# The Gram matrix from high and low fp32r parts, and LN1's normalisation on ScalarE from the second batch on

## The chip, the cores and the metric

The kernel runs on one core of a Trainium2 chip. The metric is the device time of one execution in microseconds (us). The numbers of the profile come from one execution recorded by the hardware profiler.

## The reference

Inputs are x (8 batches of 2048 tokens of 256 features), an attention with 8 heads of 64, a gated feed-forward block and six modulation rows per batch. All is float32.

```
sa, ca, ga, sb, cb, gb = (silu(c) @ wmod), six rows of 256 per batch; ga, gb pushed to |.| >= 0.25
h   = layernorm(x) * (1 + ca) + sa                        # LN1
q, k, v = split(h @ w_qkv + b_qkv)
s   = einsum('bhld,bhle->bhde', q, k) / 8                 # 64 x 64 per head, summed over the tokens
o   = v @ softmax(s)   per head;  o = o @ w_fc + b_fc + h
x   = x + ga * (layernorm(o) * gamma + beta)
h   = layernorm(x) * (1 + cb) + sb                        # LN2
xr, xk = mixes of h with h of the token before
x   = x + gb * sigmoid(xr W_r') * (relu(xk W_k')**2 W_v')
```

The attention is over features, so all that the scores need of a batch is the Gram matrix G = Z^T Z of z, the normalised x with a last column that stands for the bias. Scores, softmax and the product with w_fc are folded into one 256 x 256 matrix M per batch, and the attention output of a token is z M.

## The kernel before, in words

A batch is cut in four tiles of 512 tokens (`CH = 4`), a tile in four blocks of 128 (`NT = 4`). Every engine has an instruction list of its own, written out by hand: a prologue with batch 0's Gram matrix, `row_steps(b)` for b = 0 to 6, `last_row(7)`. `row_steps(b)` does attention and feed-forward of batch b, and between them the LN1, transposes, Gram matrix, scores and M of batch n = b + 1. There is no planner: the order in each list is the schedule, and semaphores tie the lists together.

What the change touches, in the order of the data:

- VectorE `stats_a` takes the statistics of a tile of x, GpSimd `rstd_a` (through `layernorm_factors`, L445 to L461) makes mean and 1/std, VectorE `make_z` (L884) writes z, in two buffers. Tiles 0 and 1 of batch n + 1 are normalised at the end of `row_steps(b)`, tiles 2 and 3 in the next one.
- TensorE `turn_and_gram` transposes z into the banks `tr` (L1249) and adds the tile's part to the bank `gram` (L1256): per block an f32 matmul of 256 columns and one of 128, since the lower left quarter follows from symmetry. ScalarE copies the transposes (`copy_z_t`, L618).
- After the fourth tile ScalarE copies three quarters of G (`copy_gram`), TensorE transposes one (`turn_gram`, L1349), ScalarE copies that (`copy_gram_low`), and `gram_q` (L1359) begins the scores. Then come the softmax on VectorE, `wv_attn` (L1376; it needs `wv_aug` from GpSimd's L494 to L504), and `make_m` (L1385, added up on VectorE at L1015).

What lies around it: `attention(b, j)` (L1274) fills the banks `att`; ScalarE `squares` sums them, GpSimd `rstd_o` (L476, L478) makes 1/std, VectorE `make_x2` (L894, L899) makes the new x, `stats_2` (L905) its statistics, GpSimd `rstd_2` the factors of LN2, ScalarE `make_z2` (L699) normalises, TensorE `turn_z2` (L1291) transposes, ScalarE `copy_h2` (L661) modulates, VectorE `mix` (L919, L923) mixes, and `ffn_r` (L1307), `ffn_k` (L1324), `take_r` (L671), `take_k` (L680 to L684), `low_k` (L932), `ffn_out` (L1140 to L1142, three fp32r products) and `gate_o` (L941) follow. `attention(b, 2)` waits for `t_done` of tile 1, `turn_z2(b, j)` also for the copies of the next z tile, since both use the banks `tr`. GpSimd's list of a middle batch has, in this order, `rstd_o(b,0)`, two DMA issues, `rstd_2(b,0)`, `prep_wv(n)`, `rstd_o(b,1)`; in the prologue `centre_wv(0)` waits for `row8_b_ready`, which the end of VectorE's `rows_b` (L838 to L857) sends.

Of the kernel before, what the change touches and what calls it, by code (L numbers as in the profile page):

```python
# [24 lines left out]
F32 = mybir.dt.float32  # L25
# [8 lines left out]
def adaln_block(nc, x, w_qkv, b_qkv, w_fc, b_fc, gamma, beta, w_r, w_k, w_v, mu_r, mu_k, c, wmod, out):  # L34
# [19 lines left out]
    with ExitStack() as ctx:  # L54
# [25 lines left out]
        def att_banks(j, alone):  # L80
# [7 lines left out]
        neg_half, half, quarter, minus_one, eps_att = (  # L88
            sb(n, [P, NT]) for n in ("neg_half", "half", "quarter", "minus_one", "eps_att"))
# [43 lines left out]
        z = sb("z", [P, 2, NT, D])  # L133
        z_t = sb("z_t", [P, CH, KD, CT])
# [112 lines left out]
        ag_a_step = sem("ag_a_step")  # L247
        rs_a_ready = sem("rs_a_ready")
# [3 lines left out]
        z_t_ready = sem("z_t_ready")  # L252
        x2_rowed = [sem(f"x2_rowed{j}") for j in range(CH)]
# [170 lines left out]
        def _(pool):  # L424
            def build_constants():
# [11 lines left out]
                nc.gpsimd.memset(quarter[:], 0.25).then_inc(const_ready, 1)  # L437
                nc.gpsimd.memset(eps_att[:], EPS_ATT).then_inc(const_ready, 1)
# [3 lines left out]
                nc.gpsimd.memset(z[:, :, :, LAST:D], 1.0).then_inc(const_ready, 1)  # L442
                pool.wait_ge(const_ready, 10)

            def layernorm_factors(i, st, ag, st_done, ag_step, ready, eps):  # L445
# [66 lines left out]
            def row_steps(b, first, far):  # L512
# [73 lines left out]
        def _(act):  # L586
# [27 lines left out]
            def copy_z_t(b, j):  # L614
                i = CH * b + j
                for h in range(KD):
                    act.wait_ge(z_turned, 2 * i + h + 1)
                    nc.scalar.activation(z_t[:, j, h], tr[h][:], ACT.Copy).then_inc(z_t_ready, 1)  # L618

            def copy_gram(b):  # L620

                act.wait_ge(z_used, CH * (b + 1))
                nc.scalar.activation(g_sb[:, 0], gram[:, 0:D], ACT.Copy)
                nc.scalar.activation(g_sb[:, 1, P:D], gram[:, D:D + P], ACT.Copy).then_inc(g_up_ready, 1)

# [77 lines left out]
            def row_steps(b, first):  # L703
# [26 lines left out]
                copy_gram_low(n)  # L730
# [4 lines left out]
                make_z2(b, 3)  # L735
                exps(n)
# [47 lines left out]
            row_steps(0, True)  # L784
            with act.Fori(1, B - 1) as b:
                row_steps(b, False)
# [4 lines left out]
        def _(dve):  # L791
# [67 lines left out]
            def centre_fc():  # L859
# [4 lines left out]
                nc.vector.tensor_scalar(fc_mean[:], fc_mean[:], 1.0 / D, None, ALU.mult).then_inc(fc_step, 1)  # L864
                dve.wait_ge(fc_step, 2)
# [11 lines left out]
            def make_z(b, j, first=False):  # L877
# [8 lines left out]
                ins.then_inc(z_ready, 1)  # L886

# [130 lines left out]
            def row_steps(b, first, far):  # L1018
# [18 lines left out]
                mix(b, 0)
# [29 lines left out]
                if far:  # L1067
                    stats_a(n + 1, 3)
# [427 lines left out]
```

## Time and profile before

| what | value |
|---|---|
| median of 3 runs | 707.41 us (706.69 to 708.01) |
| the profiled execution's own time | 705.8 us |
| its span, first to last instruction | 704.2 us |
| PE busy in the stretches 0 to 75, each middle batch, 647 to the end | 65.6 of 75; 81.0 of 82; 45.2 of 57 us |
| distance of the same instruction in two middle batches | 82.05 us |
| mean granted TensorE clock | 0.991 |
| VectorE, ScalarE, GpSimd busy in a middle batch's 82 us | 63.5, 48.4, 47.7 us |

Matmuls overlap in the pipeline, so a group's duration in the lists is longer than its pace. The pace is the distance from one start to the next. An idle time in brackets is that of the engine ahead of the row, with what ended it.

### The profile page before, as it was taken

How to read it: one execution, taken by the hardware profiler on the slowest of the kernel's cores; microseconds unless marked ns; L12 is line 12 of the kernel's file. 1: busy time of each engine (PE TensorE's matmuls, PEld its weight loads, DVE VectorE, ACT ScalarE, POOL GpSimd, SP SyncE). 2: the span in 40 equal slices, each digit the busy share in tenths (PEclk: the TensorE clock that was granted, in tenths of full speed). 3: DMA queues.
4: the chain of work that ended last, by engine and by line, in shares of the span. 5: the costliest groups of instructions: out<-in, count | busy, mean ns of one | idle time of the engine just before them, and what ended most of it. 6: DMA issues, size and time to landing. Idle time of an engine off the chain costs nothing.

```text
span 704.2 us, 11623 instructions
## 1 busy us (share of the span) xinstructions
PE 676.1 (96%) x3584; PEld 548.0 (78%) x3584; DVE 524.8 (75%) x1030; ACT 392.8 (56%) x871; POOL 389.5 (55%) x809
## 2 busy tenths in 40 slices
PE   7988999999999999999999999999999999998896
PEld 6767787978788887887879787888878878786665
DVE  4784898768878687868877688786878588467853
ACT  1434575556655475474755565554754747546552
POOL 5172885567275663586455672756635864326530
PEclk9999999999999999999999999999999999999999
DMA  9759255675846375573926657563755629616225
GB/s 317 220 166 210 90 158 91 130 163 113 194 86 146 120 158 118 97 177 89 217 77 133 162 117 184 89 151 111 165 116 92 124 57 199 117 29 153 30 31 89
DMA packets 90984, 93.02 MB, mean 132 GB/s; under 512 B 4224, under 2 KB 89000, under 8 KB 90960
## 3 DMA queue, kind: packets, MB, share of 16 engines
q0 software_dynamic: 33264, 33.03, 31.9%
q1 hardware_dynamic: 55344, 55.97, 24.9%
q10 hardware_dynamic: 2352, 3.73, 1.5%
q8 instruction: 11, 0.18, 0.1%
q14 instruction: 13, 0.11, 0.1%
HBM read 42.84 MB, written 33.10 MB: 108 GB/s over the span
## 4 chain that ended last, share of the span: by engine, by line
PE 34%; POOL 26%; issue 21%; DVE 9%; ACT 6%; DMA 2%; POOLq 1%; DVEq 0%; SPq 0%
PE work L1307 6%; PE att L1274 5%; PE gram L1256 5%; PE work L1324 4%; POOL x L483 4%; POOL ag L461 2%; ACT z L699 2%; POOL wv_aug L494 2%; PE tr L1249 2%; POOL ag_a L461 2%; DVE t_buf L894 2%; DVE mx L923 2%; POOL wv_aug L497 2%; PE gram L1385 2%; POOL rs_o L478 2%
## 5 line engine op out<-in xcount | busy, mean ns | idle before, releaser
L1274 PE MATMUL att<-m_sb,z_t 128*128 128x256 f32 x496 | 112.9, 381 | 8.4 <-DVE t_buf L894 7.6
L1274 PEld LDWEIGHTS att<-m_sb,z_t 128*128 128x128 f32 x496 | 92.4, 190 | 24.9 <-issue 13.7
L1324 PE MATMUL work<-mx,w_k_t 128*128 128x512 f32 x236 | 106.2, 592 | 0.0
L1307 PE MATMUL work<-w_r_t,mx 128*128 128x256 f32 x464 | 105.0, 379 | 0.0
L894 DVE SCALAR_TENSOR_TENSOR t_buf<-att,rs_o,g_row 128x256 f32<-128x256 f32 x124 | 51.4, 477 | 64.4 <-POOL rs_o L478 64.4
L1307 PEld LDWEIGHTS work<-w_r_t,mx 128*128 128x128 f32 x464 | 86.1, 190 | 10.4
L699 ACT ACTIVATE z<-x,ag 128x256 f32<-128x256 f32 x128 | 66.5, 598 | 48.6 <-POOL ag L471 48.6
L1256 PE MATMUL gram<-z 128*128 128x256 f32 (+1 forms) x512 | 89.7, 329 | 0.0
L449 POOL TENSOR_TENSOR ag<-st 128x4 f32<-128x4 f32 x32 | 18.6, 582 | 125.5 <-DVE st L905 125.5
L652 ACT ACTIVATE sq<-att 128x256 f32<-128x256 f32 x124 | 45.9, 382 | 72.4 <-PE att L1274 72.4
L1256 PEld LDWEIGHTS gram<-z 128*128 128x128 f32 x512 | 80.4, 192 | 6.7
L923 DVE SCALAR_TENSOR_TENSOR mx<-t_buf,mu_col,h2t 128x512 f32<-128x512 f32 x120 | 82.2, 748 | 1.1
L1324 PEld LDWEIGHTS work<-mx,w_k_t 128*128 128x128 f32 x236 | 44.9, 190 | 44.0 <-issue 42.5
L1140 PE MATMUL work<-wvf_lo,k_hi 128*128 128x256 f32 x248 | 77.1, 311 | 0.0
L1142 PE MATMUL work<-wvf_hi,k_lo 128*128 128x256 f32 x248 | 69.7, 281 | 0.0
L1141 PE MATMUL work<-wvf_hi,k_hi 128*128 128x256 f32 x248 | 69.5, 280 | 0.0
L932 DVE TENSOR_TENSOR k_lo<-work,k_hi 128x512 fp32r<-128x512 f32 x61 | 41.9, 690 | 36.6 <-ACT k_hi L684 35.5
L671 ACT ACTIVATE y<-work 128x512 f32<-128x512 f32 x58 | 34.5, 595 | 59.4 <-PE work L1307 59.3
L483 POOL DMA_DIRECT2D x<-in_L_attn_x_dram x32 | 55.0, 1821 | 0.0
L884 DVE TENSOR_SCALAR z<-x_in,ag_a 128x255 f32<-128x255 f32 x128 | 50.0, 453 | 6.1 <-POOL ag_a L461 4.1
L661 ACT ACTIVATE h2t<-tr,mod_now 128x512 f32<-128x512 f32 x64 | 46.2, 776 | 12.1 <-PE tr L1291 12.1
L510 POOL DMA_DIRECT2D out_dram<-y x29 | 39.3, 1355 | 18.5 <-DVE y L941 17.6
(176 smaller groups left out, 1373.8 us busy)
## 6 DMA issues: line engine op xcount, KB each, us to landing
x_in<-in_L_attn_x_dram SPq DMA_DIRECT2D x32, 512.0 KB, 4.9
x<-rows SPq DMA_DIRECT2D x32, 512.0 KB, 3.5
x<-in_L_attn_x_dram POOLq DMA_DIRECT2D x32, 512.0 KB, 9.4
out_dram<-x SPq DMA_DIRECT2D x31, 512.0 KB, 4.8
out_dram<-y POOLq DMA_DIRECT2D x29, 512.0 KB, 6.0
rows<-row_scratch SPq DMA_DIRECT2D x16, 128.0 KB, 4.9
rows<-row_scratch SPq DMA_DIRECT2D x8, 256.0 KB, 3.8
wqkv_sb<-in_L_attn_w_qkv_dram ACTq DMA_DIRECT2D x1, 1536.0 KB, 10.0
```

The costliest lines, as they stand in the source:

```text
L483: nc.gpsimd.dma_start(x2[:, j], x_v[b, j], accum_op=ALU.add).then_inc(x2_filled[j], 16)
L699: ins = nc.scalar.activation(z2[:, t], x2[:, j, t], ACT.Identity, bias=ag_2[:, s, 1, t:t + 1], scale=ag_2[:, s, 7, t:t + 1])
L884: ins = nc.vector.tensor_scalar(z[:, j % 2, t, 0:LAST], x_in[:, j, t, 0:LAST], ag_a[:, j, 3, t:t + 1], ag_a[:, j, 7, t:t + 1], ALU.subtrac ...
L894: ins = nc.vector.scalar_tensor_tensor(t_buf[:, t], att_banks(j, alone)[t // 2][:, (t % 2) * D:(t % 2 + 1) * D], rs_o[:, s, t:t + 1], g_ro ...
L923: ins = nc.vector.scalar_tensor_tensor(dst[:, h], dif[:, h], mu_col[:, n, h:h + 1], prev[:, h], ALU.mult, ALU.add)
L1140: mm(dst, s_hi, m_lo, start=start, stop=False)
L1141: mm(dst, s_hi, m_hi, start=False, stop=False)
L1142: return mm(dst, s_lo, m_hi, start=False, stop=stop)
L1256: ins = mm(gram[:, k * D:(k + 1) * D - k * P], z[:, j % 2, t, k * P:(k + 1) * P], z[:, j % 2, t, k * P:D], start=(j == 0 and t == 0 and k ...
L1274: ins = mm(att_banks(j, alone)[q][:, (t % 2) * D:(t % 2 + 1) * D], z_t[:, j, k, t * P:(t + 1) * P], m_sb[:, k], start=(k == 0), stop=(k == ...
L1307: ins = mm(r_banks(alone)[q][:, (t % 2) * D:(t % 2 + 1) * D], mixed(j, alone)[0][:, ch, tile], w_r_t[:, ch], start=(ch == 0), stop=(ch == ...
L1324: ins = mm(k_banks(alone)[dh][:], w_k_t[:, ch, rows_dh], mixed(j, alone)[1][:, ch], start=(ch == 0), stop=(ch == KD - 1))
```

## The change

TensorE now forms G in two fp32r products, z_hi^T z_hi and z_lo^T z_hi, with all 256 columns in each. z is doubled by factors in `rstd_a`, z_hi is z/2 rounded to fp32r (ScalarE, `high_z`), z_lo = z - 2 z_hi (VectorE, `low_z`, one buffer). The bank then holds A = (z_hi + z_lo)^T z_hi; half of A goes to `g_sb`, four transposes lay the transposed halves in the bank, and VectorE `whole_gram` adds both. Batch 0's four tiles and batch 1's tiles 0 and 1 are still made by VectorE in the prologue; from batch 1's tile 2 on z is made by ScalarE (`make_z`). The lists change in these places:

```
 # GpSimd: rstd_a ends with two more small operations, and its tile 0 moves ahead of rstd_2(b, 3)
             def rstd_a(b, j):
+                layernorm_factors(i, ..., rs_a_step, 0.25, sixteenth)
+                nc.gpsimd.tensor_tensor(ag[:, 0], ag[:, 3], minus_one[:], ALU.mult)
+                nc.gpsimd.tensor_tensor(ag[:, 1], ag[:, 0], ag[:, 7], ALU.mult).then_inc(rs_a_ready, 1)
 # ScalarE
+            def make_z(b, j):            # 4 x ACTIVATE Identity 128x255, bias and scale per token
+            def high_z(b, j):            # ACTIVATE Copy 128x1024, scale 0.5, fp32r out
             def copy_gram(b):
-                nc.scalar.activation(g_sb[:, 0], gram[:, 0:D], ACT.Copy)
-                nc.scalar.activation(g_sb[:, 1, P:D], gram[:, D:D + P], ACT.Copy)
+                nc.scalar.activation(g_sb, gram[:], ACT.Copy, scale=0.5)      # 128x512
-            def copy_gram_low(b): ...
 # ScalarE's row_steps, + is new:
   squares(b,0) copy_z_t(n,0) prep_base_qk(n) take_r(b-1,3) take_k(b-1,3) make_z2(b,0) squares(b,1)
   +make_z(n,2) copy_z_t(n,1) +high_z(n,2) copy_h2(b,0) squares(b,2) copy_z_t(n,2) +make_z(n,3)
   take_r(b,0) make_z2(b,1) take_k(b,0) +high_z(n,3) copy_h2(b,1) squares(b,3) make_z2(b,2)
   copy_z_t(n,3) copy_gram(n) copy_h2(b,2) take_r(b,1) take_k(b,1) copy_gq(n) make_z2(b,3)
   +make_z(n+1,0) exps(n) take_r(b,2) take_k(b,2) copy_pv(n) +high_z(n+1,0) copy_h2(b,3)
   +make_z(n+1,1) +high_z(n+1,1)
 # VectorE
+            def low_z(b, j):             # SCALAR_TENSOR_TENSOR 128x1024, both inputs in SBUF
+                dve.wait_ge(z_ready, i + 1)
+                dve.wait_ge(z_hi_ready, i + 1)
+                wait_past(dve, z_used, i)
+            def whole_gram(b):           # TENSOR_TENSOR 128x512, after gram_turned
 # VectorE's row_steps, + new, - gone:
   take_g prep_now make_x2(b,0) stats_2(b,0) prep_qk(n) low_k(b-1,3) -make_z(n,2) +low_z(n,1)
   make_x2(b,1) stats_2(b,1) +low_z(n,2) mix(b,0) gate_o(b-1,3) take_wvf make_x2(b,2) stats_2(b,2)
   low_k(b,0) -make_z(n,3) mix(b,1) +low_z(n,3) gate_o(b,0) make_x2(b,3) +whole_gram(n)
   +stats_a(n+1,0) mix(b,2) low_k(b,1) stats_2(b,3) -stats_a(n+1,0) gate_o(b,1) softmax_dif(n)
   stats_a(n+1,1) softmax_norm(n) -make_z(n+1,0) -make_z(n+1,1) stats_a(n+1,2) low_k(b,2)
   make_m(n) mix(b,3) +low_z(n+1,0) stats_a(n+1,3) gate_o(b,2)
 # VectorE's prologue, from batch 0's fourth tile on
             make_z(0, 3, first=True)
+            low_z(0, 2)
             prep_qk(0)
+            low_z(0, 3)
+            mean_fc()
+            whole_gram(0)
             rows_b()
             centre_fc()
             stats_a(1, 0)
 # ScalarE's prologue: a high_z ahead of each copy_z_t(0, j); j = 2 comes after prep_base_qk(0) and two weight copies
 # TensorE
-                for t in range(NT):
-                    for k in range(KD):
-                        ins = mm(gram[:, k * D:(k + 1) * D - k * P], z[:, j % 2, t, k * P:(k + 1) * P], z[:, j % 2, t, k * P:D], ...)
+                pe.wait_ge(z_hi_ready, i + 1)
+                for n, rows_z in enumerate((hi, z_lo)):
+                    if n == 1:
+                        pe.wait_ge(z_lo_ready, i + 1)
+                    for t in range(NT):
+                        for k in range(KD):
+                            ins = mm(gram[:, k * D:(k + 1) * D], rows_z[:, t, k * P:(k + 1) * P], hi[:, t], ...)
                 ins.then_inc(z_used, 1)
             def turn_gram(b):
-                nc.tensor.transpose(gram[:, D + P:2 * D], g_sb[:, 0, P:D], ident[:]).then_inc(gram_turned, 1)
+                for k in range(KD):
+                    for m in range(KD):
+                        ins = nc.tensor.transpose(gram[:, k * D + m * P:...], g_sb[:, m, k * P:(k + 1) * P], ident[:])
```

## Rows read from the trace of the kernel before

**Rows 1.** Page, part 1: busy time, share of the span, instructions.

```profile
PE 676.1 (96%) x3584; PEld 548.0 (78%) x3584; DVE 524.8 (75%) x1030; ACT 392.8 (56%) x871; POOL 389.5 (55%) x809
```

**Rows 2.** Waits of PE, whole span: total us, times, longest.

```profile
PE att L1274 <- DVE t_buf L894: 7.6, 8, 1.1
```

**Rows 3.** Timeline of PE, a middle batch: start, us, operation, [idle before].

```profile
402.47 3.69 PE L1274 MATMUL att<-m_sb,z_t 128*128 128x256 f32 x16 [1.03 <-DVE t_buf L894]
...
423.08 0.28 PE L1142 MATMUL work<-wvf_hi,k_lo 128*128 128x256 f32 x1
423.20 0.28 PE L1140 MATMUL work<-wvf_lo,k_hi 128*128 128x256 f32 x1
...
423.56 1.03 PE L1249 MATMUL tr<-ident,z 128*128 128x128 f32 x8
424.43 2.78 PE L1256 MATMUL gram<-z 128*128 128x256 f32 x16
427.05 1.04 PE L1291 MATMUL tr<-ident,z 128*128 128x128 f32 x8
```

**Rows 4.** Timeline of DVE, end of one batch and start of the next.

```profile
456.27 0.69 DVE L1015 TENSOR_TENSOR m_sb<-gram,res 128x512 f32<-128x512 f32 x1 [1.45 <-PE gram L1385]
...
460.79 1.39 DVE L874 BATCH_NORM_STATS2 st_a<-x_in 128x6 f32<-128x256 f32 x4
...
466.57 1.66 DVE L894 SCALAR_TENSOR_TENSOR t_buf<-att,rs_o,g_row 128x256 f32<-128x256 f32 x4 [2.47 <-POOL rs_o L478]
...
470.85 1.27 DVE L980 SCALAR_TENSOR_TENSOR wqk_aug<-wqkv_sb,d_now,wqk_aug 128x1024 f32<-128x1024 f32 x1
```

**Rows 5.** Timeline of POOL over the same stretch.

```profile
441.93 0.19 POOL L469 TENSOR_TENSOR ag<-ag,minus_one 128x4 f32<-128x4 f32 x1
...
442.35 0.20 POOL L449 TENSOR_TENSOR ag_a<-st_a 128x4 f32<-128x4 f32 x1
...
462.26 0.20 POOL L449 TENSOR_TENSOR ag_a<-st_a 128x4 f32<-128x4 f32 x1 [6.03 <-DVE st_a L874]
...
465.26 0.19 POOL L476 TENSOR_TENSOR ve_o<-ssq,eps_att 128x4 f32<-128x4 f32 x1
...
471.01 1.17 POOL L449 TENSOR_TENSOR ag<-st 128x4 f32<-128x4 f32 x1 [1.87 <-DVE st L905]
...
476.73 2.40 POOL L494 TENSOR_TENSOR wv_aug<-wv_t,rows 128x1024 f32<-128x1024 f32 x1
```

**Rows 6.** Timeline of DVE around mix(b,1).

```profile
421.08 1.22 DVE L919 TENSOR_TENSOR t_buf<-h2t 128x1024 f32<-128x1024 f32 x1
...
424.99 1.28 DVE L941 SCALAR_TENSOR_TENSOR y<-y,work 128x512 f32<-128x512 f32 x2
```

**Rows 7.** Timeline of ACT: the copy that mix(b,1) waits for.

```profile
419.05 1.44 ACT L661 ACTIVATE h2t<-tr,mod_now 128x512 f32<-128x512 f32 x2
```

**Rows 8.** Timeline of ACT, prologue.

```profile
16.77 1.08 ACT L618 ACTIVATE z_t<-tr 128x512 f32<-128x512 f32 x2 [11.80 <-issue]
...
23.88 1.15 ACT L691 ACTIVATE wqk_aug<-wqk_last,neg_d 128x1024 f32<-128x1024 f32 x1 [0.47 <-DVE d_now L973]
```

**Rows 9.** Timeline of DVE, prologue: rows_b begins.

```profile
30.18 0.41 DVE L845 TENSOR_SCALAR mx<-work 8x256 f32<-8x256 f32 x1
```

**Rows 10.** Timeline of POOL, prologue.

```profile
35.59 2.35 POOL L494 TENSOR_TENSOR wv_aug<-wv_t,rows 128x1024 f32<-128x1024 f32 x1 [12.91 <-DVE mx L857]
...
48.06 0.31 POOL L504 COPY wv_aug<-vb_col 128x4 f32<-128x4 f32 x1
```

**Rows 11.** Timeline of PE, prologue.

```profile
36.56 3.67 PE L1359 MATMUL att<-wqk_aug,g_sb 128*128 128x512 f32 x8 [0.41 <-ACT g_sb L628]
...
48.53 2.74 PE L1376 MATMUL att<-wv_aug,attn 128*128 128x256 f32 x8
```

**Rows 12.** Timeline of PE, last batch.

```profile
650.12 1.09 PE L1291 MATMUL tr<-ident,z 128*128 128x128 f32 x8 [1.89 <-ACT z L699]
...
661.00 1.92 PE L1291 MATMUL tr<-ident,z 128*128 128x128 f32 x8 [2.90 <-ACT z L699]
```

More of the change, by code:

```diff
@@ L712, in row_steps @@
                     make_z2(b, 0)
+                    make_z(n, 2)
                 else:
@@ L717, in row_steps @@
                     squares(b, 1)
+                    make_z(n, 2)
                     copy_z_t(n, 1)
+                high_z(n, 2)
                 copy_h2(b, 0)
@@ L721, in row_steps @@
                 copy_z_t(n, 2)
+                make_z(n, 3)
                 take_r(b, 0)
@@ L724, in row_steps @@
                 take_k(b, 0)
+                high_z(n, 3)
                 copy_h2(b, 1)
@@ L735, in row_steps @@
                 make_z2(b, 3)
+                if far:
+                    make_z(n + 1, 0)
                 exps(n)
@@ L740, in row_steps @@
                 take_k(b, 2, halves=(1,))
+                if far:
+                    high_z(n + 1, 0)
                 copy_h2(b, 3)
+                if far:
+                    make_z(n + 1, 1)
+                    high_z(n + 1, 1)
             def last_row(b):
@@ L770, in _ @@
             load_more()
+            high_z(0, 0)
             copy_z_t(0, 0)
+            high_z(0, 1)
             copy_z_t(0, 1)
@@ L783, in _ @@
             copy_pv(0)
-            row_steps(0, True)
-            with act.Fori(1, B - 1) as b:
-                row_steps(b, False)
+            high_z(1, 0)
+            high_z(1, 1)
+            row_steps(0, True, True)
+            with act.Fori(1, B - 2) as b:
+                row_steps(b, False, True)
+            row_steps(B - 2, False, False)
             last_row(B - 1)
@@ L857, in rows_b, with mean_fc @@
                 nc.vector.tensor_scalar(row8[:, GB + 2 * D:NR], tmp8[:, 2], 0.5, None, ALU.mult).then_inc(row8_b_ready, 1)
-            def centre_fc():
+            def mean_fc():
                 dve.wait_ge(wfc_loaded, 16)
@@ L1027, in row_steps @@
                     stats_a(n, 3)
+                    low_z(n, 1)
                     make_x2(b, 1)
                     stats_2(b, 1)
-                    make_z(n, 2)
                 else:
@@ L1033, in row_steps @@
                     low_k(b - 1, 3)
-                    make_z(n, 2)
+                    low_z(n, 1)
                     make_x2(b, 1)
                     stats_2(b, 1)
+                low_z(n, 2)
                 mix(b, 0)
@@ L1045, in row_steps @@
                 low_k(b, 0)
-                make_z(n, 3)
                 mix(b, 1)
+                low_z(n, 3)
                 gate_o(b, 0)
                 make_x2(b, 3)
+                whole_gram(n)
+                if far:
+                    stats_a(n + 1, 0)
                 mix(b, 2)
@@ L1106, in _ @@
             stats_a(0, 3)
+            low_z(0, 1)
             make_z(0, 2, first=True)
@@ L1123, in _ @@
             make_m(0)
+            low_z(1, 0)
             dve.wait_ge(mod_col_ready, 2)
```

80 lines of the change are left out of this document (54 added, 26 removed).

## The prediction, made before the changed kernel was seen

> **What bounds the kernel now.** I read the page's busy shares first: TensorE is busy 96% of the span [rows 1], so by shares alone the kernel is bound by TensorE, and less matmul work should be less time. Then TensorE's waits: nearly all there is inside the batches is one wait of about 1 us, eight times, of attention(b, 2) for t_buf of tile 1 [rows 2]. So one dependency chain is already as long as TensorE's work beside it, and what TensorE saves beside that chain it will spend waiting. That is why I read the timelines next.
>
> I call M the end of TensorE's make_m, as VectorE sees it (456.27), and A the start of attention(b, 2) (402.47, and one period of 82.05 later 484.52) [rows 3, 4]. M to A is 28.25 us, A to M 53.8 us.
>
> The chain from M to A, with nothing idle in it: VectorE adds up M at once, runs mix(b,3), and takes stats_a(n+1,3) at 460.79 [rows 4]. GpSimd waited 6.03 us for these statistics (462.26). It makes their factors by 465.26, then rs_o for the next batch [rows 5], for which VectorE's t_buf at 466.57 waits [rows 4]. Statistics go back to GpSimd at 471.01, whose factors for LN2 take until 476.73, where prep_wv begins [rows 5]. Then follow rs_o of tile 1, t_buf, and A, 7.8 us after 476.73. Beside this chain TensorE does 27.2 us of work and waits 1.03 us.
>
> **The change part by part.**
>
> TensorE. Consecutive fp32r matmuls of 256 columns start 0.12 us apart [rows 3], as in ffn_out, whose operands and shapes are of the same kind. A tile's Gram part becomes 16 of them, 1.88 us. It took 2.62 (424.43 to 427.05), so 0.74 less per tile, 23.7 us in 32 tiles. Transposes pace at 0.11 us (eight in 0.87, from 423.56) [rows 3]. turn_gram has four in place of one, 0.33 more per batch, 2.6 us in all. If nothing waited, the change would be worth 21 us.
>
> M to A. Two Gram parts lie here, 1.48 us less work, but on the side that waits: worth 0. The chain gets longer:
> - low_z(n+1,0) now stands between mix(b,3) and stats_a(n+1,3). VectorE is busy without a gap from M on, so it counts whole. The nearest row is L980, same operation, same 1024 elements, both inputs in SBUF: 1.27 us [rows 4], and since neighbours overlap a little I take 1.2. Bounds: 0.7 (half the size of L919's 1.22 [rows 6], were some mode faster) to 2.4, should GpSimd hold it up once.
> - rstd_a has two more small operations. In rstd_2 the same two take from 441.93 to 442.35: 0.42 us [rows 5], ahead of rs_o, on the chain.
> - low_z(n,1) runs while GpSimd ends rstd_2(b,0). There GpSimd's first operation took 1.17 us beside VectorE's L980, in place of 0.20 (471.01 against 462.26 [rows 5]). make_z stood in that place before, so only part is new: I take 0.3, between 0 and 1.2.
>
> The first is shown by rows. For the rule behind it, the Trainium skill, page "SBUF — State Buffer", section "Who interferes with whom", says that VectorE with two SBUF inputs locks out a GpSimd operation that reads SBUF until it ends. The 1.17 us agrees. By the page alone the third item would be up to 1.2, and the sum below up to 5.4 us more.
>
> So M to A becomes 28.25 + 1.2 + 0.42 + 0.3 = 30.2. TensorE has 25.75 us of work there and waits 4.4 us, in pieces: out3 for low_k(b-1,3) (pushed back by the chain's 1.6 us, while TensorE is early), turn_z2(b,0) for the copies of z tile 1, which now stand on ScalarE behind make_z(n,2), and attention. ScalarE's own path there (make_z2 2.0, squares 1.4, make_z 2.0, copy 1.1, then the transposes 0.9, with 0.2 of latencies) takes 7.6 us from the same start as GpSimd's last 7.8. It is nearly as late, and doesn't decide.
>
> A to M. Two Gram parts (1.48 less) and turn_gram (0.33 more). If nothing waited it would be 52.65. But low_z(n,3) stands behind mix(b,1), and this waits for copy_h2(b,1). That copy ended at 420.49 [rows 7], and gets 0.3 later (0.74 earlier by TensorE, 1.05 later by high_z(n,3) ahead of it on ScalarE). mix started at 421.08 only since make_z was in its way, and ended at 425.07 [rows 6]. It will end at about 424.9, low_z at 426.1. The high product of tile 3 is done before 424.7, so TensorE waits 1.5 us, the low one (0.94) ends at 427.1. Before, the Gram part ended at 427.05 [rows 3]. Both savings are gone, and turn_gram's 0.33 with 0.1 for the longer copy stays: A to M is 54.25. Here the wait costs 1.5, with bounds of 0.5 and 2.5 (mix by one of its instructions earlier or later). I find nothing later that is late: whole_gram is done 5 us before gram_q wants it, and low_k(b,1) moves with TensorE.
>
> A period is 84.45 in place of 82.05, **+2.4**. Six periods lie between attention(0,2) and attention(6,2): +14.4. Behind the last there is one A to M more, +0.45.
>
> The prologue. ScalarE issues DMAs until 16.77 [rows 8], so high_z(0,0) ends at 17.9, low_z at 19.2, and the first Gram part some 2 us later than before. high_z(0,2) stands behind prep_base_qk and two weight copies. These began at 23.88 when VectorE was ready [rows 8], and will about 3.4 later. That puts high_z(0,2)'s end at 32.3, low_z(0,2)'s at 33.6. low_z(0,3) comes behind prep_qk (3.2) at 37.9, and the last low product ends at 39.0. Copy 0.6, transposes 0.45, mean_fc meanwhile, whole_gram 0.7: gram_q starts at 41.2 and not 36.56 [rows 11], +4.6. What costs more: rows_b, which ran from 30.18 [rows 9] to 35.1, stands now behind whole_gram, so it ends at 46.0. GpSimd's centre_wv had waited for just this, 12.91 us, and began at 35.59 [rows 10]. It takes 4.3, two rstd_a 3.3 each, then bias_wv at 48.06 [rows 10]. Now these follow one another from 46.0: wv_aug is ready at 57.3. wv_attn started at 48.53 [rows 11] and will at 57.4: **+8.9**. All that follows (M of batch 0, the DMAs of the next rows, attention) moves along. In batch 0's first tiles low_z(1,1) costs GpSimd some 0.3 more. Bounds: 4.6, if GpSimd were no constraint, to 12, if centre_fc and centre_wv slow each other.
>
> Sum: 8.9 + 0.3 + 14.4 + 0.45 = 24.0 us on the profiled execution's 705.8 (span 704.2 and 1.6 around it): 729.8. The median of the runs is 1.6 above that execution: **731.4**.
>
> **The rivals.**
>
> 1. Faster: TensorE stays the bound. If low_z took no place on the chain (GpSimd and VectorE overlapping more than the timelines allow), the periods would fall to 82.05 - 2.6 = 79.4. With the prologue as above: 707.4 - 6 x 2.6 + 9 = 701. It decides from the point where M to A is under 26.8 us. For it: 96% busy. Against: the 1.03 us wait, which says that TensorE has no part in that stretch's length. With the prologue's delay absorbed too it would be 692.
>
> 2. The clock falls in the longer waits. After an idle 1.89 us eight transposes took 1.09 as ever; after 2.90 us they took 1.92 [rows 12]. So TensorE ran the latter at the lower level, 1.2 GHz, at first. The new waits before turn_z2(b,0) are near 2.3 us. Should the clock fall there, attention(b,2) and what follows it lose about 1.7 us per batch: 731.4 + 6 x 1.7 = 742.
>
> 3. Only part of the chain is as I say: low_z(n+1,0) is partly hidden, or low_z(n,3) comes in time. Then the period is 82.05 to 83.3 and the sum 717 to 724.
>
> 4. The change doesn't do what it says: fp32r at f32's pace. It would take 16 x 0.22 = 3.5 us a tile, and the stretch A to M would grow by some 2 more: 745. The 0.12 us of ffn_out [rows 3] speaks against it.
>
> **How the numbers follow.** Forecast 0.55, rival 1 0.07, rival 2 0.18, rival 3 0.17, rival 4 0.03. The range, 717 to 742, takes in rival 3 and rival 2, with the bounds of the prologue. About 0.2% is the least that a measurement of this kernel can tell. Slower 0.91, same 0.02, faster 0.07.
>
> **What would show it.** L1256 x1024 with starts 0.12 us apart. The period between attentions about 84.4. The waits of PE in a middle batch near 6 us, of which 1.5 inside the Gram part of tile 3 for low_z (VectorE, scalar_tensor_tensor of 1024), and attention(b,2) released by t_buf as before. VectorE's stats_a(n+1,3) about 5.7 us after m_sb, in place of 4.5. wv_attn of batch 0 near 57, released by wv_aug or attn. Granted clock stays near 0.99. Wrong it would be if the waits of attention(b,2) stay at 1 us or if the period is under 82.

## The result, and the profile of the changed kernel

The changed kernel is slower: 751.59 us in the median of 4 runs (751.5 to 752.91), against 707.05 (706.55 to 708.01) beside it, ratio 1.0633 with a 95% interval of 1.0614 to 1.0651. I had forecast 731.4, between 717 and 742. The sign was right and the size was not: +24.0 us forecast, +45.8 in the span (704.2 to 750.0).

Page of the changed kernel, part 1 (busy time, share of the span, instructions), which answers to [rows 1]:

```profile
PE 671.2 (89%) x3608; PEld 539.9 (72%) x3608; DVE 522.2 (70%) x966; ACT 470.8 (63%) x991; POOL 438.2 (58%) x874
```

TensorE's work did shrink (676.1 to 671.2 us), though by far less than the span grew. So the loss is waiting. TensorE's waits in the changed kernel (total us, times, longest), which answer to [rows 2]:

```profile
PE tr L1362 <- ACT z_t L629: 18.5, 6, 3.1
PE gram L1327 <- DVE z_lo L937: 10.9, 9, 1.8
PE work L1207 <- DVE k_lo L991: 9.7, 6, 1.7
PE tr L1362 <- ACT z L722: 7.7, 5, 2.9
PE att L1450 <- POOL wv_aug L514: 6.0, 1, 6.0
PE work L1395 <- ACT y L694: 3.8, 1, 3.8
PE gram L1327 <- ACT z_hi L650: 3.6, 2, 3.3
PE tr L1316 <- ACT h2t L684: 3.4, 1, 3.4
```

The one wait of a middle batch, 1.03 us before attention(b, 2), has become three: 3.1 us at the transposes of z2 (L1362), 1.1 at the low Gram product of tile 3 (L1327), 1.7 at out3's first matmul (L1207). The rows with "1 time" belong to the prologue and batch 0.

M, VectorE's addition of `m_sb`, occurs once per batch, so its eight times cut every execution of this study into the same four stretches (us; the third in brackets also per batch). The clock is the mean granted one.

| kernel | start to M(0) | M(0) to M(1) | M(1) to M(7) | M(7) to the end | clock |
|---|---|---|---|---|---|
| before | 55.8 | 72.2 | 492.3 (82.06) | 83.9 | 0.991 |
| changed | 67.0 | 82.9 | 516.3 (86.04) | 83.8 | 0.979 |
| difference | +11.2 | +10.7 | +23.9 (+4.0) | -0.1 | |

In the forecast's own marks (starts of attention(b, 2)) it is +11.5 before the first, +13.6 in batch 0's row, +20.1 over five middle periods, +0.6 behind them. Forecast were 9.2, 2.4, 12.0 and 0.45.

**A middle batch.** Timeline of TensorE in the changed kernel (start, us, operation, [idle before]). It answers to [rows 3], one batch on:

```profile
415.42 1.20 PE L1327 MATMUL gram<-z_hi 128*128 128x256 f32 x8
416.45 1.12 PE L1327 MATMUL gram<-z_hi,z_lo 128*128 128x256 f32 x8
417.41 3.61 PE L1378 MATMUL work<-w_r_t,mx 128*128 128x256 f32 x16
...
438.59 1.97 PE L1362 MATMUL tr<-ident,z 128*128 128x128 f32 x8 [3.09 <-ACT z_t L629]
440.35 4.39 PE L1345 MATMUL att<-m_sb,z_t 128*128 128x256 f32 x16
...
462.23 1.19 PE L1327 MATMUL gram<-z_hi 128*128 128x256 f32 x8
464.55 1.22 PE L1327 MATMUL gram<-z_hi,z_lo 128*128 128x256 f32 x8 [1.13 <-DVE z_lo L937]
```

A tile's Gram part takes 1.99 us (415.42 to 417.41), against 2.62, so fp32r did bring what the pace of 0.12 us promised. The transposes behind the wait take 1.97 us in place of 1.04, and 16 attention matmuls 4.39 in place of 3.69.

VectorE on the chain from M on, which answers to [rows 4]:

```profile
408.66 0.69 DVE L1074 TENSOR_TENSOR m_sb<-gram,res 128x512 f32<-128x512 f32 x1 [1.45 <-PE gram L1459]
...
413.17 1.22 DVE L937 SCALAR_TENSOR_TENSOR z_lo<-z_hi,z 128x1024 fp32r<-128x1024 f32 x1
414.31 1.40 DVE L917 BATCH_NORM_STATS2 st_a<-x_in 128x6 f32<-128x256 f32 x4
...
420.84 1.66 DVE L953 SCALAR_TENSOR_TENSOR t_buf<-att,rs_o,g_row 128x256 f32<-128x256 f32 x4 [3.21 <-POOL rs_o L488]
...
429.48 1.22 DVE L937 SCALAR_TENSOR_TENSOR z_lo<-z_hi,z 128x1024 fp32r<-128x1024 f32 x1
```

GpSimd over the same stretch, which answers to [rows 5]:

```profile
415.79 0.20 POOL L455 TENSOR_TENSOR ag_a<-st_a 128x4 f32<-128x4 f32 x1 [6.95 <-DVE st_a L917]
...
419.52 0.20 POOL L486 TENSOR_TENSOR ve_o<-ssq,eps_att 128x4 f32<-128x4 f32 x1 [0.25 <-issue]
...
425.28 1.17 POOL L455 TENSOR_TENSOR ag<-st 128x4 f32<-128x4 f32 x1 [1.87 <-DVE st L964]
...
429.49 2.10 POOL L467 TENSOR_TENSOR ag<-ag,neg_half 128x4 f32<-128x4 f32 x1
...
432.00 2.40 POOL L504 TENSOR_TENSOR wv_aug<-wv_t,rows 128x1024 f32<-128x1024 f32 x1
```

From M to `stats_a`: 5.65 us, before 4.52 (+1.13, forecast 1.2). From the statistics' first operation to `ve_o`: 3.73, before 3.00 (+0.73, forecast 0.42: two operations and 0.25 of issue). From `rstd_2`'s first operation to `wv_aug`: 6.72, before 5.72 (+1.0, forecast 0.3): the pow at 429.49 lasts 2.10 us, beside low_z from 429.48 on; in the kernel before it lasted 1.22. The Trainium skill, "SBUF — State Buffer", section "Who interferes with whom", says that a VectorE instruction with two SBUF inputs contends with a GpSimd instruction that reads SBUF, and the 2.10 us agrees. The sum, 2.86, is within 0.03 us the growth of M to A where the clock held: 28.25 to 31.14 (495.21 to 526.35).

**Batch 0's row.** Timeline of ScalarE in the changed kernel:

```profile
87.78 2.08 ACT L641 ACTIVATE z<-x_in,ag_a 128x255 f32<-128x255 f32 x4 [3.42 <-POOL ag_a L474]
...
103.27 2.08 ACT L641 ACTIVATE z<-x_in,ag_a 128x255 f32<-128x255 f32 x4 [8.54 <-POOL ag_a L474]
105.25 1.06 ACT L694 ACTIVATE y<-work 128x512 f32<-128x512 f32 x2
```

In this row alone GpSimd makes the factors of z tiles 2 and 3 late: tile 3's stand behind `rstd_2(0,1)` and `rstd_o(0,2)` and end at 103.2. These eleven small operations took 7.3 us (95.90 to 103.2) beside VectorE's work, where the nine of the kernel before took 3.1 (86.21 to 89.27). VectorE made these two tiles in the kernel before at 76.32 and 92.07 and waited for no factors. ScalarE waits 3.42 and 8.54 us. `copy_h2(0,0)` is queued behind the first of these waits and `take_r(0,0)` behind the second, and TensorE waits 3.42 and 3.77 us for them.

**The prologue.** Timelines of GpSimd and of TensorE in the changed kernel, which answer to [rows 10] and [rows 11]:

```profile
46.30 3.14 POOL L504 TENSOR_TENSOR wv_aug<-wv_t,rows 128x1024 f32<-128x1024 f32 x1 [18.10 <-issue]
...
58.41 0.19 POOL L514 COPY wv_aug<-vb_col 128x4 f32<-128x4 f32 x1
```

```profile
41.45 3.67 PE L1433 MATMUL att<-wqk_aug,g_sb 128*128 128x512 f32 x8 [0.83 <-issue]
...
58.74 3.75 PE L1450 MATMUL att<-wv_aug,attn 128*128 128x256 f32 x8 [6.04 <-POOL wv_aug L514]
```

gram_q began at 41.45 (forecast 41.2), `centre_wv` at 46.30 (46.0), wv_attn at 58.74 (57.4).

### The profile page after: what moved, and what is told of

It reads as the page before. It is cut to its first block, busy times and chain, and to the rows that moved or that the text cites. A ratio compares the mean times of both kernels' runs of the same rounds, so it can differ in the third digit from the quotient of the medians.

```text
span 750.0 us, 11880 instructions
## 1 busy us (share of the span) xinstructions
PE 671.2 (89%) x3608; PEld 539.9 (72%) x3608; DVE 522.2 (70%) x966; ACT 470.8 (63%) x991; POOL 438.2 (58%) x874
## 3 DMA queue, kind: packets, MB, share of 16 engines
q10 hardware_dynamic: 2352, 3.73, 1.4%
## 4 chain that ended last, share of the span: by engine, by line
POOL 28%; PE 24%; issue 22%; ACT 15%; DVE 7%; ACTq 2%; POOLq 1%; DMA 1%; DVEq 0%
PE work L1378 5%; PE att L1345 4%; ACT z L722 4%; POOL ag_a L467 4%; POOL ag L467 3%; PE work L1395 3%; POOL x L493 2%; DVE mx L982 2%; ACT z L641 2%; POOL ag_a L455 2%; PE gram L1327 2%; ACT h2t L684 2%; PE tr L1362 2%; ACT sq L675 1%; ACT work L705 1%
## 5 line engine op out<-in xcount | busy, mean ns | idle before, releaser
L1345 PE MATMUL att<-m_sb,z_t 128*128 128x256 f32 x496 | 115.7, 387 | 2.8 <-DVE t_buf L953 1.5
L1345 PEld LDWEIGHTS att<-m_sb,z_t 128*128 128x128 f32 x496 | 94.7, 195 | 19.8 <-issue 7.7
L1378 PEld LDWEIGHTS work<-w_r_t,mx 128*128 128x128 f32 x464 | 86.2, 191 | 11.6 <-DVE y L1000 1.0
L1207 PE MATMUL work<-wvf_lo,k_hi 128*128 128x256 f32 x248 | 76.5, 308 | 9.7 <-DVE k_lo L991 9.7
L455 POOL TENSOR_TENSOR ag_a<-st_a 128x4 f32<-128x4 f32 x32 | 18.7, 586 | 82.8 <-DVE st_a L917 82.8
L641 ACT ACTIVATE z<-x_in,ag_a 128x255 f32<-128x255 f32 x104 | 54.0, 601 | 12.0 <-POOL ag_a L474 12.0
L1362 PE MATMUL tr<-ident,z 128*128 128x128 f32 x256 | 35.6, 284 | 26.2 <-ACT z_t L629 18.5
L1207 PEld LDWEIGHTS work<-wvf_lo,k_hi 128*128 128x128 f32 x248 | 46.7, 188 | 14.5 <-DVE k_lo L991 12.1
L1362 PEld LDWEIGHTS tr<-ident,z 128*128 128x128 f32 x256 | 30.2, 146 | 34.6 <-ACT z_t L629 19.7
```

Of the source, the lines that this page charges most:

```text
L641: ins = nc.scalar.activation(z[:, j % 2, t, 0:LAST], x_in[:, j, t, 0:LAST], ACT.Identity, bias=ag_a[:, j, 1, t:t + 1], scale=ag_a[:, j, 7, ...
L1207: mm(dst, s_hi, m_lo, start=start, stop=False)
L1345: ins = mm(att_banks(j, alone)[q][:, (t % 2) * D:(t % 2 + 1) * D], z_t[:, j, k, t * P:(t + 1) * P], m_sb[:, k], start=(k == 0), stop=(k == ...
L1362: ins = nc.tensor.transpose(tr[h][:, t * P:(t + 1) * P], z2[:, t, h * P:(h + 1) * P], ident[:])
L1378: ins = mm(r_banks(alone)[q][:, (t % 2) * D:(t % 2 + 1) * D], mixed(j, alone)[0][:, ch, tile], w_r_t[:, ch], start=(ch == 0), stop=(ch == ...
```

## The experiments

Stretches of the experiments, as in the table above, with the median of the runs, and the ratio to the kernel before with its interval. "before" beside them was 706.4, 705.84 and 706.08 in the three groups.

| run | start to M(0) | M(0) to M(1) | per batch to M(7) | clock | median | ratio |
|---|---|---|---|---|---|---|
| a_first | 70.2 | 77.6 | 87.1 | 0.958 | 750.14 | 1.0605 (1.0567 to 1.0643) |
| a_early | 66.9 | 73.7 | 86.2 | 0.977 | 744.29 | 1.0553 (1.0531 to 1.0575) |
| a_lowz0 | 66.8 | 82.9 | 86.2 | 0.966 | 752.66 | 1.0656 (1.0637 to 1.0675) |
| a_lowz3 | 68.7 | 81.8 | 85.6 | 0.961 | 746.05 | 1.0548 (1.0522 to 1.0574) |
| a_port | 67.0 | 82.8 | 85.4 | 0.972 | 747.75 | 1.0591 (1.0571 to 1.061) |
| a_rsa3 | 68.7 | 82.8 | 82.3 | 0.979 | 728.38 | 1.0312 (1.0294 to 1.0329) |
| a_bias | 63.6 | 84.8 | 86.4 | 0.966 | 751.87 | 1.0631 (1.059 to 1.0672) |
| a_gramonly | 67.8 | 80.7 | 90.5 | 0.948 | 776.62 | 1.0993 (1.0975 to 1.1011) |
| b_actz | 56.0 | 87.6 | 86.9 | 0.979 | 750.72 | 1.0639 (1.0622 to 1.0657) |
| b_actz2 | 60.4 | 81.7 | 82.6 | 0.983 | 720.91 | 1.0199 (1.0166 to 1.0233) |
| b_rsa3 | 56.9 | 71.7 | 80.8 | 0.991 | 698.44 | 0.9893 (0.9876 to 0.991) |
| a_best2 | 65.2 | 74.8 | 81.7 | 0.978 | 717.13 | 1.0165 (1.0144 to 1.0186) |

The names with `a_` start from the changed kernel, those with `b_` from the one before. a_gramonly and b_actz are the two halves of the change, b_actz2 mends b_actz, a_best2 puts several moves together, and each of the others moves one thing in the lists. All keep the whole computation. The stretches and the clock are those of the profiled execution, the median is that of all runs.

**Batch 0's row: a_first and a_early.** The theory: tile 3's factors hold ScalarE there.

```
 # a_first, GpSimd's first row
+    rstd_a(n, 2); rstd_a(n, 3)
     rstd_2(b, 1); rstd_o(b, 2)
-    rstd_a(n, 3)
 # a_early: stats_a(1, 2), stats_a(1, 3) to VectorE's prologue, ahead of make_m(0);
 #          rstd_a(1, 2), rstd_a(1, 3) to the end of GpSimd's prologue
```

> The changed kernel (751.6 us), with only GpSimd's list in batch 0's row altered: rstd_a(1,3) directly behind rstd_a(1,2), ahead of rstd_2(0,1) and rstd_o(0,2). Theory F (ScalarE's make_z(1,3) waits 8.5 us for factors that GpSimd makes late, and holds take_r(0,0) behind it): the factors come at about 92 instead of 103, the wait is gone, the distance from attention(0,2) to attention(1,2) falls from 96.0 to about 88, the time to about 743. Rival (the first row is long because VectorE and GpSimd have more to do in it, whatever the order): within 2 us of 751.6.

> The changed kernel with batch 1's tiles 2 and 3 handled early: their statistics (VectorE) and factors (GpSimd) are moved out of batch 0's row into the prologue's end, where both engines idle for over 6 us. Theory F (batch 0's row is long because ScalarE, which now makes z, waits 3.4 and 8.5 us for these factors): attention(0,2) to attention(1,2) falls from 96.0 us to 86, the time to about 742. Rival (the row is long for other reasons, as that the earlier order of the factors brought only 1.5 us in the median): over 748.

a_first took 5.4 us out of the row (82.9 to 77.6) and gave most of it back: 87.1 us per batch at clock 0.958, with 4.1 to 5.8 us for the 16 matmuls of attention(b, 2) in all six middle batches (3.69 at full clock). The expected 743 was missed, and the median, 750.14, lies where the rival had it, though the row itself did not stay. a_early took out 9.3, and now the row is within 1.5 us of the one in the kernel before. TensorE's waits for y and h2t are gone, and the time fell by 7.3 us, to 744.29 (742 expected). a_early makes the factors early and also takes their work out of the row, so by itself it doesn't tell lateness from load. a_first takes nothing out of the row. It is shown, then, that late factors cost ScalarE, and the row, at least 5.4 us of its 10.7. That most of the 9.3 is lateness too is argued: the kernel before has the same factors in this row, and it takes 72.2 us.

**The chain out of M: a_rsa3 and b_rsa3.** Behind `rstd_o(b, 1)` GpSimd waits 4.47 us for VectorE's statistics, in the changed kernel. The factors of tile 3 fit there, and `make_z(n, 3)` wants them only later.

```
 # GpSimd's list of middle batches, the same edit on the changed kernel and on the one before
     prep_wv(n); rstd_o(b, 1)
+    rstd_a(n, 3)
     rstd_2(b, 1)
 ...
     rstd_a(n + 1, 2)
-    rstd_a(n + 1, 3)
```

> The changed kernel with GpSimd's rstd_a(n+1,3) taken from the end of the row and put behind rstd_o(b,1) of the next, where GpSimd idles 4.4 us. VectorE's list is as it was, low_z(n+1,0) in its place. Theory (stats_a and rstd_a of tile 3 stand on the chain from m_sb to attention(b,2) only because rstd_o(b,0) is queued behind them): t_buf(b,0) comes 3 us sooner, that stretch falls from 31.7 to 28.5 us, the period from 85.4 to about 82.2, the time to 730 to 733. Rival (something else releases t_buf(b,0)): no change.

> The kernel before, with GpSimd's rstd_a(n+1, 3) moved from the end of a row to the place behind rstd_o(b, 1) of the next. Theory R (the chain from M through stats_a and rstd_a to ve_o also ends last in part of the old kernel, in the 1.03 us for which the transposes of z2 wait): that wait goes, the period falls from 82.05 to about 81.0, seven rows give 7 us, 699 us. Rival (TensorE is the bound in the old kernel and the wait is filled by another): 705 to 707 us.

Both came true, a_rsa3 with a little more than forecast (728.38 for 730 to 733). In the changed kernel the batch fell from 86.04 to 82.3 us, the total by 23 us. Where the clock held, M to A fell from 31.14 to 27.66, by 3.5 us; the rest of the batch's gain is clock. `ve_o` no longer waits for statistics. Timeline of GpSimd in a_rsa3:

```profile
406.44 0.20 POOL L486 TENSOR_TENSOR ve_o<-ssq,eps_att 128x4 f32<-128x4 f32 x1 [6.74 <-ACT sq L675]
...
412.76 1.16 POOL L455 TENSOR_TENSOR ag<-st 128x4 f32<-128x4 f32 x1 [1.79 <-DVE st L964]
```

`ve_o` stands 7.1 us behind M (399.31) in place of 10.9, and its releaser is now ScalarE's sum of squares. TensorE's waits of a_rsa3 at the same places as above:

```profile
PE gram L1327 <- DVE z_lo L937: 9.7, 9, 1.3
PE tr L1362 <- ACT z_t L629: 9.0, 6, 1.5
```

With it the wait at z2's transposes is 1.5 in place of 3.1, and out3's is gone. In the kernel before, the same edit removed the wait of middle batches altogether (it stood at attention(b, 2), not at z2's transposes as the expectation has it), and TensorE is busy 80.00 of 80 us there (400 to 480). Left of it are one wait in batch 0's row and one in the last batch. TensorE's waits in b_rsa3, the line that answers to [rows 2]:

```profile
PE att L1274 <- DVE t_buf L894: 0.8, 2, 0.6
```

b_rsa3 is the fastest kernel of this study: 698.44 us, 1.1% under the kernel before.

**The terms of the chain, one by one: a_lowz0, a_port, a_lowz3.**

```
 # a_lowz0, VectorE            # a_port, VectorE                   # a_lowz3, VectorE
+ stats_a(n + 1, 3)            + prep_now(n); low_z(n, 1)          + low_z(n, 3)
  low_z(n + 1, 0)                ...                                 mix(b, 1)
- stats_a(n + 1, 3)            - low_z(n, 1), ahead of make_x2(b,1) - low_z(n, 3)
```

> The changed kernel with low_z(n+1,0) and stats_a(n+1,3) swapped on VectorE. Theory (VectorE's 1.14 us stand on the chain from m_sb to attention(b,2)): that stretch falls from 31.7 to 30.5 us in a middle batch, six times, so about 745. Rival (ScalarE's path make_z2, squares, make_z, copy_z_t sets attention(b,2), the rest is slack): no change of the period, 751.

> The changed kernel with low_z(n,1) of the middle rows moved from behind low_k(b-1,3) to behind prep_now(n), where VectorE idles 3.2 us. Theory (low_z with two inputs in SBUF holds up the end of GpSimd's rstd_2(b,0), whose power operation took 2.10 us against 1.0): rstd_2(b,0) takes 5.7 us instead of 6.7, about 6 us off in all, 745.5. It may cost up to 0.3 us per batch where it stands now, beside rstd_a(n+1,3). Rival (the longer power operation has another cause, ScalarE or the DMA issues): rstd_2(b,0) still 6.7 us, 751.

> The changed kernel with low_z(n,3) ahead of mix(b,1), where VectorE idles 1.6 us. Theory (TensorE's wait of 1.13 us inside tile 3's Gram part comes from low_z standing behind mix): that wait is gone and nothing else gets late, 7 x 1.1 off, about 744. Rival (the wait reappears at ffn_r(b,1) or gram_q, since mix and the copy of G come no earlier): 750 to 752.

a_lowz0 was a miss: 752.66 for 745. Timelines of VectorE and of GpSimd in a_lowz0:

```profile
413.64 1.40 DVE L917 BATCH_NORM_STATS2 st_a<-x_in 128x6 f32<-128x256 f32 x4
414.96 1.21 DVE L937 SCALAR_TENSOR_TENSOR z_lo<-z_hi,z 128x1024 fp32r<-128x1024 f32 x1
```

```profile
415.12 1.11 POOL L455 TENSOR_TENSOR ag_a<-st_a 128x4 f32<-128x4 f32 x1 [5.59 <-DVE st_a L917]
...
419.70 0.20 POOL L486 TENSOR_TENSOR ve_o<-ssq,eps_att 128x4 f32<-128x4 f32 x1 [0.25 <-issue]
```

The statistics come 1.14 us sooner after M (4.51 us for 5.65). But now low_z runs while GpSimd makes their factors, and GpSimd's first operation lasts 1.11 us where it lasted 0.20. `ve_o` gained 0.3, and so did M to A where the clock held (30.83 for 31.14). In a_port it is the same: low_z at 415.07 stretches the pow of rstd_a, `ve_o` comes 1.0 us later after M, and the other pow is back at 1.03. Timeline of GpSimd in a_port:

```profile
415.15 2.02 POOL L467 TENSOR_TENSOR ag_a<-ag_a,neg_half 128x4 f32<-128x4 f32 x1
...
427.82 1.03 POOL L467 TENSOR_TENSOR ag<-ag,neg_half 128x4 f32<-128x4 f32 x1
```

So low_z cost this chain about 1 us in each place that was tried: by its own length on VectorE, or by what it does to GpSimd's small operation. The cost moves, it doesn't go. a_port's 3.8 us come from the place where the clock fell, not from the chain: M to A is 31.03 us (31.14 at full clock in the changed kernel). TensorE waits 2.66 us at out3 there, and the granted clock behind it was 0.72 (430 to 433 us). The transposes of z2 still wait 0.45 us behind that, so it delays nothing, and attention(b, 2) takes 3.69 us in all six batches. So no middle batch is above 85.6 us, where the changed kernel has up to 87.0. The total is near the 745.5 expected, but by luck: the chain's gain isn't there. a_lowz3 took the wait for z_lo out of the middle batches, as expected (746.05 for 744). Of the 1.1 us per batch only 0.5 shows in the profiled execution, which was the slowest of the four (751.04, the others 743.45 to 746.59): at clock 0.961 its 16 matmuls of attention(b, 2) took 5.2 to 5.8 us in every middle batch.

**The two halves: a_gramonly, b_actz, b_actz2.**

```
 # a_gramonly: the changed kernel, but z by VectorE's make_z everywhere, rstd_a without the two operations
 # b_actz:     the kernel before (f32 Gram), but z by ScalarE's make_z in the places of the change
 # b_actz2 = b_actz with, in VectorE's row_steps,
+    if far: stats_a(n + 1, 0)
     mix(b, 2); low_k(b, 1); stats_2(b, 3)
-    if far: stats_a(n + 1, 0)
```

> One half of the change alone: the Gram matrix from high and low parts, with z made by VectorE everywhere, as before. Theory: the prologue's 11 us and low_z's places stay (1.1 us on the chain before rstd_a, 1.0 us of lock against rstd_2, 0.4 for tile 3), the extra operations of rstd_a and the late factors of batch 0's row go: a period of about 84.6 us, a first row of about 84, a time of about 737. Rival (the loss comes from ScalarE's make_z): under 725.

> The other half alone: the f32 Gram matrix as before, z of tiles from (1,2) on made by ScalarE in the changed kernel's places. Theory: rstd_a's two operations put 0.5 to 0.7 us on the chain per period, batch 0's row gets 8 to 11 us longer by the late factors, the prologue nearly nothing: about 722. If both halves add up, this loss and that of the Gram half give the 44.5 us together. Rival (all of the loss is the Gram half's): 707 to 710.

> As b_actz (the old f32 Gram, z made by ScalarE), with VectorE's stats_a(n+1, 0) ahead of mix(b, 2), where the change has it. Theory S (b_actz lost its time to rstd_a(n+1, 0) standing on GpSimd ahead of rstd_2(b, 3) before its statistics were there): the waits of 3.5 us for y go, period about 83, first row dearer by some 5 us, 718 us. Rival (ScalarE's longer queue ahead of take_r(b, 2) costs this by itself): 745 to 750 us.

The first two were misses, and taught the most. a_gramonly is the slowest of all. TensorE's waits in a_gramonly:

```profile
PE gram L1322 <- DVE z_lo L927: 23.7, 9, 3.2
PE att L1340 <- DVE t_buf L943: 13.9, 8, 2.1
```

With make_z and low_z both in VectorE's list, low_z of tile 3 is 3.1 us late. b_actz has none of this, and yet 86.9 us per batch. It was not a clean half: GpSimd took `rstd_a(n+1,0)` ahead of `rstd_2(b,3)` as in the change, but VectorE still took the statistics for it behind `stats_2(b,3)`, so rstd_2(b,3) waited for both. TensorE's waits in b_actz:

```profile
PE work L1342 <- ACT y L686: 25.8, 7, 4.6
```

b_actz2 mends it, by one line. The waits for y shrink to the one of 4.6 us in batch 0's row, the batch to 82.6, the total to 720.91 (718 expected; the row took 9.5 us more than before, 5 expected). So an in-order list turned one statistics operation in the wrong place into 30 us.

The four kernels together, medians: z on VectorE with the f32 Gram 706, z on ScalarE with the f32 Gram 720.9 (+15), z on VectorE with the fp32r Gram 776.6 (+71), both changed 751.6 (+45). With these lists the fp32r Gram is the expensive part. Moving z to ScalarE costs 15 us by itself, most of it in batch 0's row (81.7 for 72.2), but given low_z on VectorE it saves 25. These sums belong to the lists as they stand and not to the arithmetic: in a_gramonly low_z's late places also bring the clock down (5.3 to 6.5 us for the 16 matmuls of attention(b, 2) in every middle batch), and below the fp32r Gram runs in 717 us in another order.

**The prologue: a_bias.**

```
 # GpSimd's prologue
     rstd_a(1, 0)
+    bias_wv(0)
     rstd_a(1, 1)
-    bias_wv(0)
```

> The changed kernel with GpSimd's bias_wv(0) between rstd_a(1, 0) and rstd_a(1, 1) in the prologue. Theory P (the prologue's 6.04 us wait for wv_aug is a wait behind the two rstd_a): wv_attn(0) at 55.2 instead of 58.7, 748 us. Rival (z(1, 1) and low_z(1, 0) come later and hold the first row): 751 to 753 us.

`bias_wv(0)` ended at 55.2, as expected. wv_attn(0) began at 57.05 and not at 55.2, since TensorE was itself late by then, and M(0) came 3.4 us sooner. The total stood still: 751.87 (747.02 to 752.52), where 748 was expected. Two things took the gain back. The first is a wait for a DMA that the expectation doesn't have. Timelines of VectorE and of TensorE in a_bias:

```profile
72.28 0.15 DVE L1031 TENSOR_SCALAR neg_d<-rows 128x1 f32<-128x1 f32 x1 [6.56 <-DMA rows<-row_scratch]
...
72.42 1.65 DVE L953 SCALAR_TENSOR_TENSOR t_buf<-att,rs_o,g_row 128x256 f32<-128x256 f32 x4
```

```profile
74.22 5.38 PE L1345 MATMUL att<-m_sb,z_t 128*128 128x256 f32 x16 [3.34 <-DVE t_buf L953]
```

The DMA with batch 1's rows landed only 1.3 us sooner than in the changed kernel (there VectorE went on at 73.61), `t_buf` of tile 1 stands behind it, and TensorE waits 3.34 us for that where it waited 1.34. The second is the clock: the matmuls behind this wait took 5.38 us in place of 3.69. M(1) was 1.5 us sooner, M(5) 2.4 (492.80 for 495.21), and the two batches behind it, 87.7 and 86.3 (85.6 and 85.4 in the changed kernel), took the rest. The rival's number came true, but not its reason: low_z(1, 0) began at 64.23, sooner than in the changed kernel (67.61). TensorE's timeline in a_bias shows a loss to the clock already in the prologue:

```profile
41.86 6.30 PE L1433 MATMUL att<-wqk_aug,g_sb 128*128 128x512 f32 x8 [0.83 <-issue]
```

Eight matmuls that take 3.67 us in the changed kernel took 6.30 here, with no edit before them; the granted clock from 41.4 to 45 us was 0.50 here and 1.00 there. a_best2 has 6.10 in this place. These two ran on one chip and the other `a_` experiments, with 3.67, on two others, so the chip isn't excluded as the reason. An edit of 3 us in the prologue need not show in the total, then: what a DMA and the clock give or take is as large.

**Everything together: a_best2.** The moves of a_early, a_lowz3 and a_bias, a_rsa3's in another form, and two swaps on ScalarE.

```
 # GpSimd, middle batches              # ScalarE, middle batches
+    rstd_a(n, 3); rstd_o(b, 1)        +    squares(b, 1); make_z2(b, 0)
     prep_wv(n)                        -    make_z2(b, 0); squares(b, 1)
-    rstd_o(b, 1)                      +    copy_z_t(n, 1); make_z(n, 2)
-    rstd_a(n + 1, 3), at the end      -    make_z(n, 2); copy_z_t(n, 1)
```

> The changed kernel with these moves together: batch 1's statistics and factors of tiles 2 and 3 in the prologue; bias_wv(0) as in a_bias; rstd_a(n, 3) ahead of rstd_o(b, 1) of the next row and prep_wv(n) behind it; low_z(n, 3) ahead of mix(b, 1); ScalarE's squares(b, 1) ahead of make_z2(b, 0) and copy_z_t(n, 1) ahead of make_z(n, 2). Theory Q (the fp32r Gram is worth 4 to 5 us of TensorE per batch, and what hid it was only the order on the other engines): period about 79.5, first row about 83, 697 us. Rival (VectorE's and GpSimd's added work sets a floor, the waits come back elsewhere): period 82, 720 us or more.

717.13 us: 34 under the changed kernel, 11 above the one before, and not the 697 expected. The waits are nearly gone. TensorE's waits in a_best2:

```profile
PE tr L1362 <- ACT z_t L629: 9.6, 7, 1.6
PE att L1345 <- DVE t_buf L953: 5.5, 8, 2.8
PE work L1378 <- DVE mx L982: 3.4, 6, 0.6
```

In the middle batch from 385.06 to 466.75 TensorE waits 0.45, 0.57 and 1.50 us, 2.52 in all, so its work is 79.2 us. b_rsa3's batch, with the f32 Gram and hardly a wait, takes 80.8. The fp32r Gram is worth 1.6 us of a batch, not the 2.6 that I had in the forecast, and the remaining waits eat 2.5. The 1.6 can be read piece by piece. The four Gram parts of this batch take 1.99, 2.00, 2.16 and 2.15 us, the longer two ahead of a wait, so 8.30 against 10.48. turn_gram takes 0.33 more, and ffn_r behind the wait of 0.57 takes 3.75 in place of 3.46. Against b_rsa3 a_best2 loses 8.3 us before M(0), 3.1 in batch 0's row and 0.9 per batch.

## Why the prediction was right in sign and wrong in size

**The failed step** is the count of the periods: "Six periods lie between attention(0,2) and attention(6,2): +14.4", with batch 0's row counted as one at +2.4, and "low_z(1,1) costs GpSimd some 0.3 more" as all that is special to it. The row grew by 13.6 us. This row is 11.2 of the 21.8 us by which the forecast fell short; the five middle periods are 8.1 and the prologue 2.3. The forecast read the eight waits of [rows 2] as attention(b, 2) in every batch. Six of them are, in batches 1 to 6; the other two are attention(0, 1), 1.09 us, and the last batch's, 0.19. attention(0, 2) of the kernel before doesn't wait, so the middle batch's +2.4 had no ground in this row. And the forecast uses GpSimd's list of a middle batch alone. In the first row `rstd_a(n,3)` stands behind `rstd_2(b,1)` and `rstd_o(b,2)`. While VectorE made z that did no harm, but ScalarE's list has `take_r(0,0)` right behind `make_z(1,3)`, and of its waits of 3.42 and 8.54 us TensorE gets 3.42 and 3.77. a_first took 5.4 us of the row back by the order alone, a_early 9.3. The order in the lists alone, with no time in it, showed what would queue behind what.

**Undersized terms of the chain, five middle periods, +20.1 for +12.0.** The lock on GpSimd was 1.0 and not 0.3: I took the value near the lower bound since make_z had stood in the place, though the row with 1.17 us stood for the upper one. rstd_a's end was 0.73 and not 0.42. Together about 1 us per batch. low_z(n+1,0), at 1.13 for 1.2, and the place of the whole chain were right, as a_rsa3 shows: moving rstd_a(n,3) off it gives back 3.5 us of M to A. My account of the wait was right as well: out3 1.7, low_z(n,3) 1.1 (1.5 forecast), the rest before z2's transposes. Only that the latter (3.1) is ended by ScalarE's copy of z and not by t_buf was wrong: I had called ScalarE's path nearly as late, and it ends last.

**Rival 2, the clock, came in part.** I gave it 0.18 and 1.7 us per batch, as an alternative to the forecast. It came on top of it: behind the same wait of 3.06 to 3.09 us the 16 matmuls of attention(b, 2) took 3.69 us in three batches and 4.17, 4.39 and 5.38 in three others. The mean period is 86.04 and the undisturbed ones are 85.4 to 85.7, so it is some 0.5 us per batch, 3 us in all.

**A to M** was forecast at 54.25 and is 54.46 to 54.48 where the clock held. The argument that both savings of tile 3's side go to low_z(n,3) held to 0.2 us.

**The prologue** was +9.2 forecast, +11.5 measured. Each time up to `centre_wv` was right to 0.3 us. Its first operation lasted 3.14 us in place of 2.35 with VectorE's `centre_fc` and statistics beside it, the two rstd_a took 3.5 us each and not 3.3, and TensorE, after 6.04 us idle, took 3.75 us for wv_attn in place of 2.74, at a granted clock of 0.50 (58.7 to 62 us). No run took the prologue's terms apart: a_bias moved one of them and met the DMA and the clock.

**Rival 1**, that TensorE stays the bound, is the reading that the busy shares suggest, and I gave it 0.07. It needed M to A under 26.8 us, and M to A was 31.1. Rival 4 was refuted by the pace: 8 matmuls in 0.96 to 1.03 us. Rival 3 was refuted by the periods, 85.4 us and more for its 82.05 to 83.3.

What stays open: why the clock falls behind a 3.1 us wait in one batch and not in the next, and what the prologue's 11.5 us are made of beyond the times above.

## What to carry to other kernels

Work moved from one engine to another inherits the other's list: before pricing it, read for every stage, the first and the last too, when its inputs come and what is queued behind it. A tensor engine at 96% busy can still be led by a chain of small operations. Here one such chain was broken by moving one factor computation of nine to eleven small operations into an idle stretch, for 1.1% on the old kernel and 23 us on the new, while the arithmetic saving itself was worth 1.6 us a batch.

## What the runs showed of the hardware that I had not expected

- A 1.2 us VectorE operation with two inputs in SBUF stretched the small GpSimd operation that began beside it: 0.20 to 1.11 us for an addition, 1.01 to 2.02 or 2.10 for a pow. Moving the VectorE operation moved the cost (a_lowz0, a_port). The GpSimd operation that had begun before it was not stretched: in batch 0's row of the changed kernel a pow at 80.09, 0.59 us ahead of low_z, took 1.01 us, and the multiplication behind it 0.89 in place of 0.19.
- The same wait can cost twice. Eight transposes behind 3.1 us of idle took 1.09 us or 1.97, at the same place of different batches (granted clock 1.00 from 525.1 to 528, 0.50 from 438.6 to 441). The granted clock of the profiled executions ranged from 0.948 (a_gramonly, with the most waiting) to 0.991 (the kernel before and b_rsa3).
- A fall of the clock costs by where it lies. In a_port it fell behind out3's wait, ahead of another wait, and no batch was longer for it. In the changed kernel it fell behind the last wait ahead of attention(b, 2), and these batches took up to 87.0 us in place of 85.4 to 85.7.
